# The experts' transposes: row scaling folded into TensorE products with diagonal matrices

## The reference

```python
xg = x.reshape(bsz, H, n, d).transpose(1, 0, 2, 3).reshape(H, S, d)    # 4 quarters of 1024 tokens
def per_group(xf, lw, lb):
    combine, dispatch = top2_dispatch(xf, Wg, C)                       # C = 86 places for each expert
    h = moe_apply(xf, combine, dispatch, W1, b1)                       # 128 -> 512
    h = layer_norm(h, lw, lb)                                          # over the 512, for each token
    h = jax.nn.relu(h)
    return moe_apply(h, combine, dispatch, W2, b2)                     # 512 -> 128
out = layer_norm(out + x, ln_out_w, ln_out_b)
```

## Time and profile before

| | us |
|---|---|
| median of three runs | 1075.53 |
| the profiled execution, its own time | 1074.52 |
| its span, first to last instruction | 1072.5 |
| TensorE busy in the span | 890.3 (83%) |
| ScalarE busy | 774.8 (72%) |
| VectorE busy | 590.4 (55%) |
| GpSimd busy | 347.7 (32%) |
| mean granted TensorE clock | 0.92 of full |

### The profile page before, as it was taken

One profiled execution on the slowest core, in us unless ns is written; L12 is line 12 of the kernel. 1 busy time (PEld: TensorE's weight loads), 2 busy tenths in 40 slices (PEclk: granted clock), 3 DMA queues, 4 the chain that ended last, 5 costly groups with the idle time before them and its releaser, 6 DMA issues. The chain is left out here.

```text
span 1072.5 us, 19387 instructions
## 1 busy us (share of the span) xinstructions
PE 890.3 (83%) x6642; PEld 414.1 (39%) x6642; DVE 590.4 (55%) x1984; ACT 774.8 (72%) x1130; POOL 347.7 (32%) x335
## 2 busy tenths in 40 slices
PE   2958896849999999999999999998969899696740
PEld 2745673311222222222222223322357576366640
DVE  7589998861123454544425164333632337687877
ACT  1236655759999999999989999995566675575520
POOL 5413445662000000000000000304586677665643
PEclk9768997979999999999989999998989998898875
DMA  6000000354444121211212121264887864676441
GB/s 176 1 1 1 1 1 25 103 137 123 148 123 114 35 61 45 60 41 32 64 31 59 46 66 33 59 185 129 244 153 183 258 182 126 207 219 175 140 133 54
DMA packets 90365, 106.56 MB, mean 99 GB/s; under 512 B 12957, under 2 KB 63902, under 8 KB 90154
## 3 DMA queue, kind: packets, MB, share of 16 engines
q1 hardware_dynamic: 77512, 76.83, 23.9%
q0 software_dynamic: 11264, 27.80, 11.2%
q10 hardware_dynamic: 1506, 0.89, 0.3%
HBM read 68.90 MB, written 36.57 MB: 98 GB/s over the span
## 5 line engine op out<-in xcount | busy, mean ns | idle before, releaser
L1668 ACT ACTIVATE s_e<-s_ps 128x1024 f32<-128x1024 f32 x512 | 476.8, 1065 | 14.6 <-PE s_ps L1838 13.9
L1851 PE MATMUL s_acc<-s_e,s_v 128*32 128x512 f32 x2048 | 276.2, 612 | 0.7 <-ACT s_e L1668 0.7
L1285 POOL DMA_INDIRECT x_in<-x_tokens,rows_of x72 | 70.6, 981 | 455.7 <-DVE rows_of L1441 419.6
L1838 PE MATMUL s_ps<-qk 51*128 51x512 bf16 x1024 | 180.8, 389 | 25.3 <-ACT s_e L1668 9.7
L1838 PEld LDWEIGHTS s_ps<-qk 51*128 51x128 bf16 x1024 | 41.2, 93 | 276.7 <-ACT s_e L1668 256.9
L2187 PE MATMUL e_py<-w,qk 128*96 128x128 f32 x768 | 104.0, 284 | 0.0
L2187 PEld LDWEIGHTS e_py<-w,qk 128*96 128x96 f32 x768 | 93.4, 172 | 0.0
L2157 PE MATMUL e_ph<-w,qk 128*32 128x512 f32 x576 | 82.9, 650 | 4.4 <-ACT e_hs L2250 4.3
L2282 ACT ACTIVATE qk<-e_pn,ln_hid 128x384 f32<-128x384 f32 x96 | 63.3, 665 | 31.7 <-PE e_pn L2171 31.2
L1285 POOL DMA_INDIRECT e_ya<-y_rows,take x64 | 65.5, 1023 | 30.6 <-issue 27.3
L1851 PEld LDWEIGHTS s_acc<-s_e,s_v 128*32 128x32 f32 x2048 | 40.5, 108 | 81.3 <-issue 54.7
(11 more groups left out here) (457 smaller groups left out, 1410.6 us busy)
## 6 DMA issues: line engine op xcount, KB each, us to landing
h_rows<-e_hs SPq DMA_DIRECT2D x54, 256.0 KB, 5.0
w<-in_w SPq DMA_DIRECT2D x10, 768.0 KB, 6.0
qk<-parts_k SPq DMA_DIRECT2D x64, 96.0 KB
qk<-parts_k SPq DMA_DIRECT2D x64, 64.0 KB
h_rows<-x_res SPq DMA_DIRECT2D x16, 256.0 KB, 3.7
parts_q<-b_parts SPq DMA_DIRECT2D x16, 192.0 KB, 2.8
parts_k<-b_parts SPq DMA_DIRECT2D x16, 192.0 KB, 2.8
qk<-parts_q SPq DMA_DIRECT2D x64, 48.0 KB
```

The source lines that it names most:

```text
L1285: nc.gpsimd.indirect_dma_start(dst, None, rows, bass.IndirectOffsetOnAxis(ap=idx, axis=0), compute_op=op).then_inc(R["landed"][k % FLIGHT] ...
L1668: nc.scalar.activation(E[g % 4][:, 2 * pair:2 * pair + 2, :], pS[BUFFER["score", 2 * g + pair]][:].rearrange("p (a s) -> p a s", a=2), ACT ...
L1838: last = nc.tensor.matmul(pS[BUFFER["score", 2 * g + pair]][:, a * CH:(a + 1) * CH], K[c % 2][rows, pair, j * P:(j + 1) * P], Q[c % 2][row ...
L1851: last = nc.tensor.matmul(acc[hu % 2][32 * h:32 * h + 32, :], V4[c % 2][:, j, h, :], E[g % 4][:, h, :], start=j == 0, stop=j == TB - 1)
```

## The change

The three tiles of a block are no longer multiplied by their rows' inverse roots. In place of that, VectorE multiplies the 128x128 identity matrix by the inverse roots of each tile, which gives a diagonal matrix, and TensorE multiplies each piece of the tile with it: the piece is the stationary operand, as it was for the transposition, and the diagonal matrix moves through in place of the identity. The result is the transposed and scaled piece. The instruction is now a plain product and no longer a transposition. There are six diagonal matrices, two sets of three, so VectorE waits, before it writes a set, until the four groups of the block two before have run (`hn_mm`). Three of the matrices are a new tile `e_dg`, two lie in the space of `qk`, one in that of `l_wo`.

```diff
+        DG = sb("e_dg", [P, 3, P])
+        diagonals = [DG[:, i, :] for i in range(3)] + [kept.take(P) for i in range(2)] + [R["wo"][:]]
+        diagonal = lambda t: diagonals[t % (2 * TPB)]
...
                 for j in range(TPB):
-                    tr = nc.tensor.transpose(pN[k % 2][:, j * P:(j + 1) * P],
-                                             row(m * TPB + j)[:, c * P:(c + 1) * P], ident[:])
+                    tr = mm(pN[k % 2][:, j * P:(j + 1) * P], row(m * TPB + j)[:, c * P:(c + 1) * P],
+                            diagonal(m * TPB + j), start=True, stop=True)
                 tr.then_inc(hn_mm, 1)
...
                 c.run(nc.vector.reciprocal(r1[:, ts], r1[:, ts]))
+                if m >= 2:
+                    v.wait_ge(hn_mm, FC * (m - 1))
                 for t in range(m * TPB, (m + 1) * TPB):
-                    y = nc.vector.tensor_scalar(row(t), row(t), r1[:, t % NT:t % NT + 1], None, ALU.mult)
+                    y = nc.vector.tensor_scalar(diagonal(t), ident[:], r1[:, t % NT:t % NT + 1], None, ALU.mult)
                 y.then_inc(n_done, 1)
```

## The result

The changed kernel took 1083.51 us (median of five runs, 1081.66 to 1084.16) against 1075.53 before in the same session: ratio 1.0079, 95% interval 1.0055 to 1.0103, so 5.9 to 11.1 us more. The forecast was 1085, with 1074 to 1097 as its range. The profiled execution took 1084.16 us, span 1082.0.

What follows compares the result with a forecast made beforehand. The bound was taken to change by stretch among TensorE, GpSimd's gathers and VectorE. Terms -1.5+5.1+0+1.9-0.5+2.4+3.4 = +10.8 us on the profiled 1074.52 gave 1085.3 us; range 1074 to 1097, own range 1080 to 1091.

Steps and rivals of the forecast that it cites:

- +0.34 us a group: TensorE, all 96 groups: three products take 0.67 us where three transpositions took 0.33; 33 us of TensorE in all.
- The new wait: VectorE's scaling must wait for the transpositions of two blocks before; these have nearly always run, so cost 0.
- Stage 1: 784 to 808: added groups vanish in a 3.90 us transfer wait; TensorE idles less and keeps its clock, -1.5 us.
- Stage 2: 808 to 836: TensorE is full, 15 groups stand ahead of the result at 836.16, +5.1 us.
- Stage 3: To 922: 24 groups' 8.2 us fall into 9.7 us of TensorE idling while GpSimd sets the pace, 0 (-1 to +4).
- rival C: A fuller TensorE falls to its lower clock less often, each such entry costing 2.7 us: 1079 us, chance 0.08.
- Stages 4 to 6: 922 to 1014.9: +1.9 to 963.5, -0.5 to 986.8, +2.4 to 1014.9, from TensorE's groups less VectorE's shorter scalings.
- VectorE's -1.2: To 963.5 and again to 1014.9: two shorter scalings on VectorE's path save 1.2 us each time.
- Stage 7: 1014.9 to the end: nine groups in a full TensorE, the first at the lower clock, +3.4 us (up to 3.9).
- A: VectorE is the bound from 922 to 1014.9, so the change is not slower: 1075.5 us or 1069.5, chance 0.18.
- B: TensorE's time comes through because its waits move with its own earlier work: +21.1 us, 1096 us, chance 0.20.
- D: A product costs no more than a transposition, one record; only VectorE's share is left: 1068 us, chance 0.03.

Runs made afterwards that it cites:

- products alone: Against the kernel before, only the mode of the 288 transpositions changes, to products with the identity; VectorE's 512-wide scaling stays: 1083.32 us, ratio 1.0080.
- the second quarter alone: Kernel before with products with diagonal matrices only in blocks 6 to 11, other blocks unchanged: 1073.9 us, ratio 0.9979.
- The third quarter's kernel: Kernel before with products with diagonal matrices only in blocks 12 to 17, other blocks unchanged: 1076.09 us, ratio 1.0011.
- The fourth quarter's kernel: Kernel before with products with diagonal matrices only in blocks 18 to 23, other blocks unchanged: 1078.32 us, ratio 1.0012.
- the five blocks: Kernel before with products with diagonal matrices only in blocks 12, 13, 17, 20 and 21: 1073.89 us, ratio 0.9976.
- filling: Extra identity transpositions in TensorE's idle time: added to the kernel before, 1072.60 us (more of them, 1075.42); added to the changed kernel, 1075.94 us.
- the first and the fourth quarter's kernels: The first: kernel before with products with diagonal matrices only in blocks 0 to 5, 1077.65 us, ratio 1.0020. The fourth: only in blocks 18 to 23.
- without the products: Kernel before with VectorE writing diagonal matrices instead of scaling rows, TensorE still transposing with the plain identity, normalisation left out: 1071.45 us, ratio 0.9965.

## Why the prediction was right, step by step

The time, its sign and that it stays within 1% came out as forecast; 1085.3 was the sum, against 1083.5. Several terms were off, and their errors partly cancel. Measured terms are differences of delays from one pair of traces, so each is worth no more than the 2 us said above; those of blocks 1, 8, 12 and 15 are read in the same way.

**Prices.** +0.34 us a group: shown, 0.67 us a group and 1.55 a period, 0.34 more than before. The 4x that the Trainium skill ("TensorE: Matmul & The Clock Gate", Terms) has for the mode would have made it +0.98; the rows after give 2x again. VectorE's 0.68 us for three: shown. The new wait: no idle time of VectorE stands ahead of a scaling in the rows after; 0 holds.

**Stage 1, -1.5.** Measured -1.2, for a wrong reason. I expected TensorE to idle only 0.6 us and to keep its clock. The rows of the change:

```profile
800.74 0.52 PE L2147 MATMUL e_px<-ident,x_in 128*128 128x128 f32 x3 [3.88 <-DMA x_in<-x_tokens,rows_of]
801.19 1.15 PE L2160 MATMUL e_ph<-w,qk 128*32 128x512 f32 x8
...
802.52 1.95 PE L2160 MATMUL e_ph<-w,qk 128*32 128x512 f32 x8
```

It idled 3.88 us as before (blocks 0 and 1 ran at the full clock and so ended no later), and the clock fell all the same, one round later: the second round took 1.95 us. From the wait's end to the next down product 9.10 us pass, 9.03 before. The 1.2 us are the landing of the transfer, which came 1.3 us sooner counted from the experts' start. In kernels still identical to the one before at this place block 1's first down product stands between -0.4 and +2.1, in products alone at -3.3. There the clock did hold, through 3.49 us of idle time: the three rounds behind it (797.71 to 799.88) took 1.07, 1.04 and 1.04 us. So what stage 1 described can happen, but not by the short idle time that I gave for it, and in the change it didn't. The measured -1.2 can't be told from 0; its size was luck.

**Stage 2, +5.1.** Block 1's first down product is at -1.2, block 5's at +4.3: +5.5 for 16 groups, 0.34 each. At the result of block 2 (842.75 against 836.16, less 2.67) it is +3.9. Right.

**Stage 3, 0.** Up to block 8 the delay grew by 1.3, then it fell by 4.1 where the wait at 885.38 and its start at the lower clock had been, and by block 12 stood at +2.0: -2.3 from block 5, below my bound of -1. TensorE's 8.2 us did fall into its waits, as the second quarter alone shows (ratio 0.9979).

Some 1.5 to 1.9 us of the fall of 4.1 are no effect of the change. The start at the lower clock at 885.38 is one execution's: in the third and fourth quarter's kernels and the five blocks', which have the same work here, the same group waited 2.82 to 3.04 us and ran at the full clock, and they fall by 1.6, 1.5 and 1.9 us between blocks 8 and 9. What is left is that the change has no wait there at all: the longer groups fill it. The next entry at the lower clock is another matter. The fourth quarter's kernel, then the change at the place of its second row:

```profile
888.10 0.55 PE L2178 MATMUL e_pn<-ident,e_hs 128*128 128x128 f32 x3 [2.82 <-ACT qk L2288]
...
917.60 1.92 PE L2160 MATMUL e_ph<-w,qk 128*32 128x512 f32 x8 [3.45 <-ACT e_hs L2256]
```
```profile
921.45 1.06 PE L2160 MATMUL e_ph<-w,qk 128*32 128x512 f32 x8 [1.54 <-ACT e_hs L2253]
```

Here the clock does differ. This round runs at the lower clock (1.86 to 1.94 us) in all seven traces with three records to a group and no filling ahead of it, behind 2.28 to 3.51 us of idle time, and at the full clock (1.06 or 1.07) behind 1.54 us in all five with six. That is rival C's mechanism, which I had at 0.08; what it gives in time one pair of traces can't tell. From block 9 to block 12 the change's delay grows by 0.5 us, and by 1.2 in the first and the fourth quarter's kernels, which are as before here.

**Stages 4 to 6, +3.8 together.** Measured: block 12 +2.0, block 15 +5.3, block 18's first group +3.4, last held-up group +4.5. So +3.3, -1.9 and +1.1, +2.5 together. The term that failed is VectorE's -1.2 in stages 4 and 6: products alone has the change's time, within 3.5 us, so nothing is seen of it. It fits that VectorE now waits 1.45 us at 1003.44, though it does so without the products too (0.94 us). That the sum still came out smaller is the filled wait again: 3.92 us at 944.63 for 4.79, 5.22 ahead of block 18 for 7.73. And one fall of the clock that I had overlooked went away: before, the eight products at 1004.17 took 1.96 us; in the change their counterparts at 1012.34 took 1.07. (The third quarter's kernel, as before at this place, took 1.07 too, so this may be the execution and not the change.) The wait for the quarter's rows grew by 1.40 us (forecast: up to 3).

**Stage 7, +3.4.** From the last held-up group to block 23's first down product 16.11 us pass after and 11.89 before: +4.2, over my bound of 3.9, since two groups behind that wait ran at the lower clock and not one. The tail takes 1.9 back: it lasts 43.78 us from there to the end of the span, 45.69 before. Before, VectorE came to the last result without idling, as its row in that trace shows:

```profile
1032.50 0.68 DVE L2344 TENSOR_TENSOR e_ys<-e_py,gate 96x512 f32<-96x512 f32 x1
```

After, it waits 1.16 us for it at 1042.17. I had left out that something else was nearly as late in the tail.

**The rivals.** A (VectorE is the bound) needed VectorE over 3 us behind TensorE at 995.66; it was level. By A the change would be 6.0 us faster than products alone; it is 0.1 +-3.5, which refutes A. B's +21 is far off: the second quarter passes on nothing. C is true in part: a fuller TensorE kept its clock at 921.45, and perhaps at 1012.34, where the kernel before had lost it. But it lost it behind three waits still (944.63, 992.99, 1022.11), and six records at the lower clock cost 1.28 us and not 0.67. C's price of 2.7 us holds for the entry at 885.38; the one at 938.40 cost 1.8 (6.2 to 944.62 for the work that took 4.4). D is refuted by the 288 added records. Of the signs, the last run of gathers starts 6.9 us later (1046.10 against 1036.49, less 2.67), in keeping with the 5 or more that I asked for. One sign of being wrong did come: VectorE idles where it was full, at 1003.44. It goes with the -1.2 that failed, and the errors of the other stages hid it in the sum.

## What to carry to other kernels

Look, before a pass moves from VectorE to TensorE, which of the two is the later at their meeting points: here VectorE already waited for TensorE at 836.16 and 1021.62 and was level with it at 995.66, and the move cost 8.5 us. Do each half of such a trade by itself first: here they gave +8.6 and -3.8 and together +8.5. The reading that fits is that the receiving engine becomes the one waited for and the relieved one idles longer; the 3.7 us by which the halves fail to add up are just inside the noise. Give an aid like the filling to both kernels before its effect is called a part of the change. The Trainium skill ("Perfetto Trace Analysis", Transposes) advises the transposition over a plain product where the operation is logically a transposition; for float32 these runs agree, 0.33 against 0.67 us for a group of three. Read a term of 1 to 2 us from one pair of traces only beside a kernel that is still the same at that place.

## What the runs showed of the hardware

- A float32 128x128 product with a new stationary operand is two records 0.112 us apart, a transposition of the same tile one; six records take 0.65 to 0.67 us in either mode.
- Transpositions raise and hold the clock: 1.00 in 850 to 928 with twice as many of them, 0.90 before and 0.95 to 0.96 in three kernels with the same work, and filling an idle stretch with transpositions kept the next group at the full clock (3.30 us for 24 records against 4.66).
- After an idle time of 3.88 us the first round of products still ran at the full clock (1.15 us at 801.19) and the one behind it at the lower (1.95 us); before, behind 3.90 us, already the first one did (1.93 us). In products alone all three rounds behind 3.49 us ran at the full clock.
- Nor does one wait always bring the lower clock: the group at 885.38 ran at it behind 2.68 us (0.90 us for three records), the same group in five other traces at the full clock behind 1.43 to 3.40 us (0.55).
- The time ahead of the experts' part varies by 6 us between executions of the same work (L1486 at 739.6 to 745.8), more than most effects measured here.
